# Nine masks and a copy in place of ten masks, and the mean subtracted inside ScalarE's squares and scalings, in a graph layer with residual and layer norm

## The chip, the cores and the metric

The kernel runs on one core of a Trainium2 chip. Five engines work side by side, each through its own list of instructions in order: PE (TensorE) multiplies and transposes, DVE (VectorE) and ACT (ScalarE) do elementwise work, POOL (GpSimd) here issues indirect DMAs (gathers and scatters), and SP (SyncE) issues the other DMAs. They wait for each other through semaphores. PE writes to PSUM, the others work from SBUF and PSUM. The metric is the time of one execution on the device in microseconds (us), as a median over runs.

## What is computed

50,000 nodes with 64 features, 25,000 edges sorted by target node, 10 edge types. All data is float32.

```
def ref(nfeat, efeat, relation_weight, res_fc_w, res_fc2_w, src, dst, etype):
    proj = einsum('ni,rio->nro', nfeat, relation_weight)
    t_r, h_r = proj[src, etype], proj[dst, etype]
    att = sum(t_r * tanh(h_r + efeat), axis=-1)
    a = softmax of att over the edges of each dst
    h_nb = segment_sum(nfeat[src] * a[:, None], dst)
    return leaky_relu((nfeat + h_nb) @ res_fc_w.T, 0.01) + leaky_relu(nfeat * h_nb @ res_fc2_w.T, 0.01)
y = x + ref(...)
return (y - mean(y)) / sqrt(var(y) + 1e-5)        # over the 64 features of a node
```

A node without edges has `h_nb` = 0, so its row needs only one product with `res_fc_w`.

## The kernel before

**Two kinds of work.** *Dense tiles*: all 50,000 rows are computed as if no node had edges, in 49 tiles of 1024 rows (128 partitions x 8 rows x 64 features = 128x512), and stored to `out`. *Edges*: the 25,000 edges lie in 196 columns of 128 and are handled in 25 steps of 8 columns (the last has 4). The rows of nodes that have edges ("finished rows") are then scattered over the dense ones.

**The loop.** Every engine runs the same loop, `s` from -1 to 28, written out by hand. In iteration `s`, PE, DVE and ACT treat: edge step `s` (transposing the gathered rows into `xT_ps`, masks, products with the weights: "quads"), edge step `e = s-1` (tanh, scores, softmax weights, running sums `es`), `f = s-2` (the two products of the output), `l = s-3` (norm of finished rows) and the dense tiles `3s+3` to `3s+5` (`D0`, `D1`, `D2`; `DP` is the last one of the iteration before). Tile 48, the last, is `D0` of iteration 15. ACT begins an iteration with the tanh of the edge step before.

**Masks and quads.** For each of the R = 10 types `r`, DVE's `mask(s, r)` (L963) writes `xm = (typ == r) * xT_ps`, 128x1024, into a ring of RM = 4; PE's `quad(s, r)` multiplies it with that type's weights, four products that add up in `t_ps` and `h_ps` over the ten types. `turn_in(s+1)` overwrites `xT_ps` when all masks of `s` are written.

**Norm of a dense tile.** PE transposes the tile (L566), ACT copies it (`dense_copy`, L712), PE multiplies (L573), ACT applies relu (`dense_relu`, L717), DVE adds (`dense_add`, L1025), sums over the 64 features (`dense_total`, L1030) and subtracts the mean (`dense_centre`, L1035). ACT squares (`dense_square`, L724: one 128x512 instruction), DVE sums (`dense_sum`, L1040). Once per iteration ACT takes the square roots of three tiles and one step of finished rows (`roots`, L777, with a table load before it and one behind it, L778), DVE inverts them (`inverse_roots`, L1047, semaphore `rec_done`), and ACT scales (`dense_norm`, L731: eight 128x64 instructions, since each row of a partition has its own factor). SP stores (L323). **Finished rows** go the same way in `final_sum`, `final_centre` (L1100), `final_square` (L783), `final_squares`, `final_out` (L790).

**POOL.** 384 gathers (L454), then, once all dense tiles are stored (`pool.wait_ge(o_stored[k], o_need(k))`), 196 scatters (L478), one gather for the node at the partitions' ends, and a last scatter (L495). Function `pace` puts waits ahead of some, so that gather number n is not issued before PE has done 14.6 n - 250 of its counted instructions (13.64 per scatter).

**SP.** Per iteration: types of the next step, edge features, loads of dense tiles (L317), stores of three tiles, the store of `es`, and 48 DMAs of single rows (L389, `rows_at`, six groups of eight) that replace some of POOL's gathers. All in one written order, so that a store also waits for the row DMAs ahead of it.

Of the kernel before, what the change touches and what calls it, by code (L numbers as in the profile page):

```python
# [5 lines left out]
ALU = mybir.AluOpType  # L6
# [17 lines left out]
RT = 2  # L24
# [5 lines left out]
RO = 3  # L30
RW = 18
# [9 lines left out]
def gnn_resnorm(nc, x, src, dst, eattr, etype, relw, resw, resw2, out):  # L41
# [55 lines left out]
    with ExitStack() as ctx:  # L97
# [9 lines left out]
        def sems(name, n):  # L107
# [35 lines left out]
        xm = sb("xm", [P, RM, COLS * P])  # L143
        ea = sb("ea", [P, RE, COLS, D])
# [49 lines left out]
        at_done = sem("at_done")  # L194
        typ_in = sems("typ_in", RT)
# [104 lines left out]
        def _(sp):  # L300
# [36 lines left out]
            def load_typ(s):  # L337
                if not 0 <= s < NS:
                    return
                wait(sp, masked, (s - RT + 1) * R)  # L340
# [162 lines left out]
        def _(pe):  # L503
# [12 lines left out]
            def turn_in(s):  # L516
# [3 lines left out]
                wait(pe, masked, s * R)  # L520
# [28 lines left out]
            def quad(s, r):  # L549
                pe.wait_ge(masked, s * R + r + 1)  # L550
                if r == 0:
                    wait(pe, prod_done, s)
                b = (s * R + r) % RM
                n = cols(s) // 2 * P
                for h in range(2):
                    pe.matmul(t_ps[h * D:(h + 1) * D, 0:n], w_rel[0:D, r, :], xm[0:D, b, h * n:(h + 1) * n],  # L556
                              start=(r == 0), stop=(r == R - 1), skip_group_check=True)
                    mm = pe.matmul(h_ps[(1 - h) * D:(2 - h) * D, 0:n], w_rel[D:P, r, :], xm[D:P, b, (1 - h) * n:(2 - h) * n],  # L558
                                   start=False, stop=(r == R - 1), skip_group_check=True)
                mm.then_inc(quad_done, 1)  # L560
# [62 lines left out]
            pe.wait_ge(setup_m, 3)  # L623
            for s in range(-1, LAST + 1):
# [45 lines left out]
                if s == NS:  # L670

                    pe.wait_ge(max_done, NS)
                    pe.wait_ge(masked, NS * R)
# [27 lines left out]
        def _(act):  # L701
# [6 lines left out]

            def dense_copy(d):
# [63 lines left out]
            def roots(s):  # L773
# [3 lines left out]
                act.activation(sd[:, s % 2, :, :], ssq[:, s % 2, :, :], ACT.Sqrt, scale=1.0 / D, bias=eps_t[:, 0:1]).then_inc(sqrt_done, 1)  # L777
# [508 lines left out]
```

## Time and profile before

| | us |
|---|---|
| median of 3 runs | 757.59 |
| lowest and highest | 756.48, 757.81 |
| the profiled execution | 757.37 |
| its span in the trace | 755.7 |
| busy in the span: DVE, POOL, PE, ACT | 628.0, 569.9, 567.3, 484.1 |
| mean granted clock of PE | 0.93 |

The profile is of one execution. Its page lists each engine's busy time, what each engine waited for ("idle before, releaser"), groups of instructions by source line, and the chain that ended last. A timeline lists instructions in order of time with start and duration; neighbours of one kind are merged (x8). An engine's successive instructions overlap a little, so that eight of 0.33 us can take 2.0 us. "PEclk" is the share of TensorE's full clock of 2.4 GHz that was granted; 0.50 is the lower level, 1.2 GHz.

### The profile page before, as it was taken

The numbers are of one execution on the slowest core, as the hardware profiler recorded it, in microseconds if no ns is written. First come the engines' busy times: TensorE is split into PE (matmuls) and PEld (weight loads), VectorE is DVE, ScalarE is ACT, GpSimd is POOL, SyncE is SP. The second block draws the span as 40 slices with busy tenths as digits, with TensorE's granted clock in tenths as the row PEclk, the third lists the DMA queues.
The fourth block names the chain that finished last, engine by engine and source line by source line (L and its number), as shares of the span: only waits on it lengthen the run. The fifth ranks groups of instructions, "written<-read, shape, count | busy, mean of one in ns | idle before, by whom it ended". The sixth has DMA issues, their size and how long they took to land. (4 is left out here: it accounts for less than half of the span.)

```text
span 755.7 us, 14910 instructions
## 1 busy us (share of the span) xinstructions
PE 567.3 (75%) x3948; PEld 310.8 (41%) x3948; DVE 628.0 (83%) x1118; ACT 484.1 (64%) x1432; POOL 569.9 (75%) x590
## 2 busy tenths in 40 slices
PE   1897888888888898888898796899988898853000
PEld 0652454454454454454454453444444443542000
DVE  2689899999999999999999999999998898862010
ACT  0376777778778788779779778655543555665040
POOL 6777777777777777777777777767777777777776
PEclk9999999999999999999999999999999999975555
DMA  4463434444434434434434424320222212100000
GB/s 120 112 188 83 122 99 138 113 110 137 124 100 138 124 96 139 124 97 141 134 85 147 113 56 123 98 77 28 76 76 74 75 37 80 45 27 18 18 18 16
DMA packets 49458, 70.44 MB, mean 93 GB/s; under 512 B 17450, under 2 KB 20966, under 8 KB 49374
## 3 DMA queue, kind: packets, MB, share of 16 engines
q1 hardware_dynamic: 30750, 52.33, 21.5%
q0 software_dynamic: 18624, 17.16, 11.0%
q8 instruction: 32, 0.52, 0.3%
q14 instruction: 52, 0.43, 0.2%
HBM read 45.61 MB, written 25.78 MB: 94 GB/s over the span
## 5 line engine op out<-in xcount | busy, mean ns | idle before, releaser
L454 POOL DMA_INDIRECT xsd<-in_x,ends_i x384 | 374.5, 975 | 118.0 <-issue 109.1
L556 PE MATMUL t_ps<-xm,w_rel 64*64 64x512 f32 (+1 forms) x1000 | 269.5, 621 | 42.0 <-DVE xm L963 41.2
L963 DVE SCALAR_TENSOR_TENSOR xm<-typ,xT_ps 128x1024 f32<-128x1024 f32 (+1 forms) x250 | 291.6, 1183 | 7.2 <-issue 7.2
L558 PE MATMUL h_ps<-xm,w_rel 64*64 64x512 f32 (+1 forms) x1000 | 269.5, 621 | 0.0
L478 POOL DMA_INDIRECT out<-out_r,row_i x196 | 192.3, 981 | 62.5 <-issue 56.7
L556 PEld LDWEIGHTS t_ps<-xm,w_rel 64*64 64x64 f32 x1000 | 52.8, 134 | 144.7 <-DVE xm L963 120.4
L573 PE MATMUL y_ps<-bd_cat,dT 128*128 128x256 f32 x392 | 97.0, 391 | 17.6 <-DVE zd L1025 14.9
L731 ACT ACTIVATE o_t<-zd,rstd 128x64 f32<-128x64 f32 x392 | 98.8, 337 | 15.4 <-DVE rstd L1047 15.3
L573 PEld LDWEIGHTS y_ps<-bd_cat,dT 128*128 128x128 f32 x392 | 71.8, 193 | 30.8 <-issue 12.9
L1005 DVE SCALAR_TENSOR_TENSOR es<-es,wd,wx 128x64 f32<-128x64 f32 x196 | 55.2, 281 | 11.2 <-DVE es L1005 0.5
L738 ACT ACTIVATE wd<-delta 128x16 f32<-128x16 f32 (+1 forms) x25 | 5.4, 216 | 88.2 <-DVE delta L993 83.8
L593 PEld LDWEIGHTS s_ps<-bd_both,uwT 128*128 128x128 f32 x224 | 29.6, 192 | 64.0 <-issue 51.9
L583 PE MATMUL tr_ps<-ident,uw 128*128 128x128 f32 x196 | 33.2, 294 | 26.4 <-DVE uw L1057 10.5
L558 PEld LDWEIGHTS h_ps<-xm,w_rel 64*64 64x64 f32 x1000 | 52.9, 134 | 0.0
L744 ACT ACTIVATE wx<-xsd,wd 128x64 f32<-128x64 f32 x196 | 52.1, 337 | 0.8
L593 PE MATMUL s_ps<-bd_both,uwT 128*128 128x128 f32 x224 | 39.8, 301 | 17.1 <-issue 17.1
L790 ACT ACTIVATE out_r<-zcf,rstd 128x64 f32<-128x64 f32 x196 | 49.1, 333 | 0.0
L583 PEld LDWEIGHTS tr_ps<-ident,uw 128*128 128x128 f32 x196 | 21.5, 145 | 65.4 <-issue 35.1
L1025 DVE TENSOR_TENSOR zd<-rd,y_ps 128x512 f32<-128x512 f32 x49 | 33.2, 677 | 9.2 <-ACT rd L717 9.2
L783 ACT ACTIVATE sqf<-zcf 128x512 f32<-128x512 f32 (+1 forms) x25 | 15.3, 613 | 39.6 <-DVE zcf L1100 39.5
L724 ACT ACTIVATE sqd<-zd 128x512 f32<-128x512 f32 x49 | 30.9, 631 | 12.6 <-DVE zd L1035 12.6
L777 ACT ACT_TABLE_LOAD x29 | 37.2, 1283 | 0.5
(155 smaller groups left out, 844.8 us busy)
## 6 DMA issues: line engine op xcount, KB each, us to landing
xsd<-in_x SPq DMA_DIRECT2D x1024, 0.2 KB
x_in<-in_x SPq DMA_DIRECT2D x48, 256.0 KB
typ<-typ_d SPq DMA_DIRECT2D x24, 512.0 KB, 4.8
out<-o_t SPq DMA_DIRECT2D x48, 256.0 KB
xsd<-in_x,ends_i POOLq DMA_INDIRECT x384
hist<-es SPq DMA_DIRECT2D x24, 256.0 KB, 2.0
ea<-in_edge_attr SPq DMA_DIRECT2D x24, 224.0 KB
out<-out_r,row_i POOLq DMA_INDIRECT x196, 2.1
```

The costliest lines, as they stand in the source:

```text
L454: pool.indirect_dma_start(xsd[:, s % RX, j, side, :], None, x[:, :], bass.IndirectOffsetOnAxis(ap=ends_i[:, side, c:c + 1], axis=0),).then ...
L478: pool.indirect_dma_start(out[:, :], bass.IndirectOffsetOnAxis(ap=row_i[:, c:c + 1], axis=0), out_r[:, s % RW, j, :], None, bounds_check=t ...
L556: pe.matmul(t_ps[h * D:(h + 1) * D, 0:n], w_rel[0:D, r, :], xm[0:D, b, h * n:(h + 1) * n], start=(r == 0), stop=(r == R - 1), skip_group_c ...
L558: mm = pe.matmul(h_ps[(1 - h) * D:(2 - h) * D, 0:n], w_rel[D:P, r, :], xm[D:P, b, (1 - h) * n:(2 - h) * n], start=False, stop=(r == R - 1) ...
L573: mm = pe.matmul(y_ps[:, j * 2 * P:(j + 1) * 2 * P], dT[:, d % 2, j * P:(j + 1) * P], bd_cat.rearrange("p k f -> p (k f)"), start=True, st ...
L583: mm = pe.transpose(tr_ps[:, j * P:(j + 1) * P], uw[:, g * QUAD + j, :, :].rearrange("p k f -> p (k f)"), ident[:, :])
L593: mm = pe.matmul(s_ps[:, YQ + j * P:YQ + (j + 1) * P], uwT[:, q // 2, k * P:(k + 1) * P], bd_both[:, :], start=True, stop=True)
L731: ins = act.activation(o_t[:, d % RO, j * D:(j + 1) * D], zd[:, d % RZ, j * D:(j + 1) * D], ACT.Copy, scale=rstd[:, s % 2, d % 3, j:j + 1])
L744: ins = act.activation(wx[:, j, :], xsd[:, e % RX, j, 0, :], ACT.Copy, scale=wd[:, e % 2, 0, j:j + 1])
L790: ins = act.activation(out_r[:, f % RW, j, :], zcf[:, f % 2, j, :], ACT.Copy, scale=rstd[:, s % 2, 3, j:j + 1])
L963: v.scalar_tensor_tensor(xm[:, (s * R + r) % RM, 0:n], typ[:, s % RT, 0:n], float(r), xT_ps[:, 0:n], ALU.is_equal, ALU.mult).then_inc(mask ...
L1005: v.scalar_tensor_tensor(es[:, e % RS, j, :], old, wd[:, e % 2, 1, j:j + 1], wx[:, j, :], ALU.mult, ALU.add).then_inc(chain_done, 1)
```

## The change

**Masks.** Since the ten masks add up to everything, sum over r of mask_r(x) W_r = x W_9 + sum over r < 9 of mask_r(x) (W_r - W_9). DVE subtracts W_9 from the other weights once in the setup (`dif_done`), writes nine masks, and ACT copies `xT_ps` whole to a new buffer `xc` (`plain`, right after tanh). PE still does ten quads; the one of `xc` stands at place 4. The first mask of a step now waits for ACT's copy.

**Norm.** `dense_centre` and `final_centre` are gone. The sums go to a table `zsum`. ACT's square becomes eight 128x64 instructions, (-64 z + sum)^2 with the sum as bias, and the root's scale goes from 1/D to 1/D^3. DVE gets a small `shifts` (-mean * rstd, 128x32), one mask after the reciprocal, and only it lets ACT go on (`rec_done`). ACT's scalings keep their number and form but take that as bias besides the scale. `zf` becomes a ring of three in place of `zcf`.

```
+            def plain(s):
+                n = cols(s) * P
+                act.wait_ge(xT_done, s + 1)
+                wait(act, quad_done, (s - 1) * R + PLAIN_AT + 1 if s > 0 else 0)
+                act.copy(xc[:, 0:n], xT_ps[:, 0:n]).then_inc(plain_done, 1)
             def dense_square(d):
-                act.wait_ge(zmid_done, d + 1)
+                act.wait_ge(zsum_done, d + 1)
                 wait(act, dred_done, d - 1)
-                act.activation(sqd[:, d % 2, :], zd[:, d % RZ, :], ACT.Square).then_inc(dsq_done, 1)
+                for j in range(DR):
+                    ins = act.activation(sqd[:, d % 2, j * D:(j + 1) * D], zd[:, d % RZ, j * D:(j + 1) * D], ACT.Square,
+                                         scale=-float(D), bias=zsum[:, d // 3 % 2, d % 3, j:j + 1])
+                ins.then_inc(dsq_done, 1)
             def dense_norm(d):
...
-                    ins = act.activation(o_t[:, d % RO, j * D:(j + 1) * D], zd[:, d % RZ, j * D:(j + 1) * D], ACT.Copy,
-                                         scale=rstd[:, s % 2, d % 3, j:j + 1])
+                    ins = act.activation(o_t[:, d % RO, j * D:(j + 1) * D], zd[:, d % RZ, j * D:(j + 1) * D], ACT.Identity,
+                                         scale=rstd[:, s % 2, d % 3, j:j + 1], bias=shift[:, s % 2, d % 3, j:j + 1])
...
             def final_square(f):
-                act.wait_ge(fsub_done, f + 1)
+                act.wait_ge(fsum_done, f + 1)
                 wait(act, red2_done, f)
-                act.activation(sqf[:, 0:cols(f), :], zcf[:, f % 2, 0:cols(f), :], ACT.Square).then_inc(fsq_done, 1)
+                for j in range(cols(f)):
+                    ins = act.activation(sqf[:, j, :], zf[:, f % RF, j, :], ACT.Square, scale=-float(D),
+                                         bias=zsum[:, f % 2, 3, j:j + 1])
+                ins.then_inc(fsq_done, 1)
...
+            v.tensor_tensor(w_rel[:, 0:RB, :], w_rel[:, 0:RB, :], w_rel[:, RB:R, :].to_broadcast([P, RB, D]), ALU.subtract).then_inc(dif_done, 1)
...
             def mask(s, r):
                 n = cols(s) * P
                 if r == 0:
-                    v.wait_ge(xT_done, s + 1)
+                    v.wait_ge(plain_done, s + 1)
...
-            def dense_centre(d):
-                v.wait_ge(zsum_done, d + 1)
-                z = zd[:, d % RZ, :].rearrange("p (j f) -> p j f", f=D)
-                v.scalar_tensor_tensor(z, zsd[:, :].unsqueeze(2).to_broadcast([P, DR, D]), -1.0 / D, z, ALU.mult, ALU.add).then_inc(zmid_done, 1)
...
-                v.reciprocal(rstd[:, s % 2, :, :], sd[:, s % 2, :, :]).then_inc(rec_done, 1)
+                v.reciprocal(rstd[:, s % 2, :, :], sd[:, s % 2, :, :]).then_inc(rstd_done, 1)
+
+            def shifts(s):
+                v.wait_ge(rstd_done, s + 1)
+                v.scalar_tensor_tensor(shift[:, s % 2, :, :], zsum[:, s % 2, :, :], -1.0 / D, rstd[:, s % 2, :, :],
+                                       ALU.mult, ALU.mult).then_inc(rec_done, 1)
```

The scaling of finished rows (`final_out`) changes as `dense_norm` does, and their sum and centring as those of the dense tiles.

How the instructions stand on ACT at the head of a dense iteration, from tanh to the exponent of the weights (`g_t` is tanh's output, `dT` the transposed tile, `h_t` the heads, `o_t` the scaled tile, `rd` the relu), before:

```order
L707 ACTIVATE g_t<-h_ps 128x512 [waits prod_done,quad_done]
L712 COPY dT<-tr_ps 128x512 [waits zadd_done,tr_in]
L756 ACTIVATE h_t<-es,rs 128x64 [waits uw_done,frec_done]
L756 ACTIVATE h_t<-es,rs 128x64 x3
L756 ACTIVATE h_t<-es,rs 128x64 [waits uw_done,frec_done]
L756 ACTIVATE h_t<-es,rs 128x64 x3
L731 ACTIVATE o_t<-zd,rstd 128x64 [waits o_stored2,rec_done]
L731 ACTIVATE o_t<-zd,rstd 128x64 x7
L717 ACTIVATE rd<-y_ps 128x512 [waits zadd_done,y_done]
L738 ACTIVATE wd<-delta 128x16 [waits den_done,delta_done]
```

and now:

```order
L722 ACTIVATE g_t<-h_ps 128x512 [waits prod_done,quad_done]
L728 COPY xc<-xT_ps 128x1024 [waits quad_done,xT_done]
L733 COPY dT<-tr_ps 128x512 [waits zadd_done,tr_in]
L780 ACTIVATE h_t<-es,rs 128x64 [waits uw_done,frec_done]
L780 ACTIVATE h_t<-es,rs 128x64 x3
L780 ACTIVATE h_t<-es,rs 128x64 [waits uw_done,frec_done]
L780 ACTIVATE h_t<-es,rs 128x64 x3
L755 ACTIVATE o_t<-zd,shift,rstd 128x64 [waits o_stored2,rec_done]
L755 ACTIVATE o_t<-zd,shift,rstd 128x64 x7
L738 ACTIVATE rd<-y_ps 128x512 [waits zadd_done,y_done]
L762 ACTIVATE wd<-delta 128x16 [waits den_done,delta_done]
```

The copy to `xc` is new in second place, and the scaling reads `shift` too. On ACT in the later half of the iteration, around the second scaling (`l` is a copy of PE's product, `sqd` and `sqf` are the squares), before:

```order
L712 COPY dT<-tr_ps 128x512 [waits zadd_done,tr_in]
L731 ACTIVATE o_t<-zd,rstd 128x64 [waits o_stored0,rec_done]
L731 ACTIVATE o_t<-zd,rstd 128x64 x7
L770 COPY l<-s_ps 128x256 [waits z1_done,y12_done]
L724 ACTIVATE sqd<-zd 128x512 [waits dred_done,zmid_done]
L783 ACTIVATE sqf<-zcf 128x512 [waits red2_done,fsub_done]
L717 ACTIVATE rd<-y_ps 128x512 [waits zadd_done,y_done]
```

and now:

```order
L733 COPY dT<-tr_ps 128x512 [waits zadd_done,tr_in]
L755 ACTIVATE o_t<-zd,shift,rstd 128x64 [waits o_stored0,rec_done]
L755 ACTIVATE o_t<-zd,shift,rstd 128x64 x7
L794 COPY l<-s_ps 128x256 [waits z1_done,y12_done]
L746 ACTIVATE sqd<-zd,zsum 128x64 [waits dred_done,zsum_done]
L746 ACTIVATE sqd<-zd,zsum 128x64 x7
L808 ACTIVATE sqf<-zf,zsum 128x64 [waits red2_done,fsum_done]
L808 ACTIVATE sqf<-zf,zsum 128x64 x7
L738 ACTIVATE rd<-y_ps 128x512 [waits zadd_done,y_done]
```

Each square is eight instructions where it was one. On DVE around the reciprocal of the roots, before:

```order
L963 SCALAR_TENSOR_TENSOR xm<-typ,xT_ps 128x1024 [waits quad_done]
L1005 SCALAR_TENSOR_TENSOR es<-es,wd,wx 128x64 [waits chain_done,wx_done] x2
L1047 RECIPROCAL rstd<-sd 128x32 [waits dmul_done,fmul_done,sqrt_done]
L963 SCALAR_TENSOR_TENSOR xm<-typ,xT_ps 128x1024 [waits quad_done]
L1035 SCALAR_TENSOR_TENSOR zd<-zsd,zd 128x512 [waits zsum_done]
L1100 SCALAR_TENSOR_TENSOR zcf<-zs,zf 128x512 [waits fmul_done,fsum_done]
```

and now:

```order
L997 SCALAR_TENSOR_TENSOR xm<-typ,xT_ps 128x1024 [waits quad_done]
L1039 SCALAR_TENSOR_TENSOR es<-es,wd,wx 128x64 [waits chain_done,wx_done] x2
L1079 RECIPROCAL rstd<-sd 128x32 [waits dmul_done,fmul_done,sqrt_done]
L997 SCALAR_TENSOR_TENSOR xm<-typ,xT_ps 128x1024 [waits quad_done]
L1083 SCALAR_TENSOR_TENSOR shift<-zsum,rstd 128x32 [waits rstd_done]
```

The two centrings behind the mask are gone, and `shift`, which ACT waits for, stands one mask behind the reciprocal.

## Rows read from the trace of the kernel before

**Rows 1.** The page: busy time, share of the span and instructions of each engine
```profile
PE 567.3 (75%) x3948; PEld 310.8 (41%) x3948; DVE 628.0 (83%) x1118; ACT 484.1 (64%) x1432; POOL 569.9 (75%) x590
```

**Rows 2.** Waits of POOL: what for, us in total, times, longest us
```profile
POOL xsd L454 <- issue: 109.1, 358, 0.3
```

**Rows 3.** Timeline of POOL: start us, us, engine, line, what; [idle before]
```profile
493.89 0.94 POOL L454 DMA_INDIRECT xsd<-in_x,ends_i  x1 [0.30 <-issue]
497.91 1.00 POOL L478 DMA_INDIRECT out<-out_r,row_i  x1 [3.07 <-DMA out<-o_t]
...
751.24 0.97 POOL L495 DMA_INDIRECT out<-out_fix,fix_i  x1 [0.30 <-issue]
```

**Rows 4.** Timeline of ACT, stages 15 and 16
```profile
468.00 2.02 ACT L731 ACTIVATE o_t<-zd,rstd 128x64 f32<-128x64 f32 x8
...
470.32 0.60 ACT L707 ACTIVATE g_t<-h_ps 128x512 f32<-128x512 f32 x1
```

**Rows 5.** Timeline of SP, stage 16
```profile
494.47 0.74 SPq L323 DMA_DIRECT2D out<-o_t  x2
```

**Rows 6.** Windows: us, busy (instructions) of each engine, PEclk, DMA share, GB/s
```profile
303.83:332.01 28.18, 23.71 (x167) 13.08 (x165) 27.57 (x48) 22.89 (x70) 21.47 (x23) 1.00 0.44 120
...
582.00:583.00 1.00, 1.00 (x8) 0.30 (x8) 1.00 (x2) 0.00 (x0) 0.70 (x2) 0.50 0.00 1
```

**Rows 7.** Timeline of ACT, stage 10, from one tanh to the next
```profile
303.09 0.60 ACT L707 ACTIVATE g_t<-h_ps 128x512 f32<-128x512 f32 x1 [0.30 <-PE h_ps L558]
...
306.93 2.00 ACT L731 ACTIVATE o_t<-zd,rstd 128x64 f32<-128x64 f32 x8
...
312.52 0.22 ACT L738 ACTIVATE wd<-delta 128x16 f32<-128x16 f32 x1 [2.89 <-DVE delta L993]
...
314.33 0.63 ACT L724 ACTIVATE sqd<-zd 128x512 f32<-128x512 f32 x1 [0.49 <-DVE zd L1035]
314.86 2.00 ACT L790 ACTIVATE out_r<-zcf,rstd 128x64 f32<-128x64 f32 x8
...
323.26 2.02 ACT L731 ACTIVATE o_t<-zd,rstd 128x64 f32<-128x64 f32 x8 [0.60 <-DVE rstd L1047]
...
331.29 0.60 ACT L707 ACTIVATE g_t<-h_ps 128x512 f32<-128x512 f32 x1 [0.30 <-PE h_ps L558]
```

**Rows 8.** Timeline of DVE, stage 10
```profile
316.48 0.68 DVE L1040 TENSOR_REDUCE ssq<-sqd 128x8 f32<-128x512 f32 x1
...
322.88 0.34 DVE L1047 RECIPROCAL rstd<-sd 128x32 f32<-128x32 f32 x1
```

**Rows 9.** Groups by form: count | busy us, mean ns of one | idle before
```profile
L963 DVE SCALAR_TENSOR_TENSOR xm<-typ,xT_ps 128x1024 f32<-128x1024 f32 x240 | 285.1, 1204 | 7.2 <-issue 7.2
...
L1035 DVE SCALAR_TENSOR_TENSOR zd<-zsd,zd 128x512 f32<-128x512 f32 x49 | 33.6, 685 | 0.6
...
L731 ACT ACTIVATE o_t<-zd,rstd 128x64 f32<-128x64 f32 x392 | 98.8, 337 | 15.4 <-DVE rstd L1047 15.3
...
L712 ACT COPY dT<-tr_ps 128x512 f32<-128x512 f32 x49 | 28.6, 584 | 12.9 <-PE tr_ps L566 12.7 <-DVE zd L1025 0.2
...
L770 ACT COPY l<-s_ps 128x256 f32<-128x256 f32 x56 | 19.8, 354 | 0.0
...
L778 ACT ACTIVATE fix<-eps_t 128x1 f32<-128x1 f32 x29 | 5.9, 203 | 0.3
...
L856 ACT ACTIVATE fix<-fix 128x1 f32<-128x1 f32 x1 | 0.3, 280 | 0.0
...
L803 ACT COPY xfix<-xsd 128x64 f32<-128x64 f32 x1 | 0.2, 244 | 0.3 <-PE xT_ps L524 0.3
```

**Rows 10.** Timeline of ACT: the tanh that ends stages 0, 4 and 14
```profile
51.58 0.60 ACT L707 ACTIVATE g_t<-h_ps 128x512 f32<-128x512 f32 x1 [0.45 <-PE h_ps L558]
...
161.78 0.60 ACT L707 ACTIVATE g_t<-h_ps 128x512 f32<-128x512 f32 x1 [0.24 <-PE h_ps L558]
...
444.01 0.60 ACT L707 ACTIVATE g_t<-h_ps 128x512 f32<-128x512 f32 x1 [0.29 <-PE h_ps L558]
```

More of the change, by code:

```diff
@@ L30 @@
 RO = 3
+RF = 3
 RW = 18
@@ L80, in gnn_resnorm, with quad_count @@
             TR_DENSE[d], tr_uses = tr_uses, tr_uses + 1
+    RB = R - 1
+    PLAIN_AT = 4
+    def quad_count(m):
+        return m // RB * R + m % RB + (2 if m % RB >= PLAIN_AT else 1)
     LATE = (ND - 1) // 3 - 2
@@ L339, in load_typ @@
                     return
-                wait(sp, masked, (s - RT + 1) * R)
+                wait(sp, masked, (s - RT + 1) * RB)
                 n = cols(s) * P
@@ L519, in turn_in @@
                     pe.wait_ge(rows_in[ROW_BLOCKS.index(s)], P * DMA)
-                wait(pe, masked, s * R)
+                wait(pe, masked, s * RB)
                 half = cols(s) // 2
@@ L547, in add_edges, with quad @@
                 mm.then_inc(eadd_done, 1)
-            def quad(s, r):
-                pe.wait_ge(masked, s * R + r + 1)
-                if r == 0:
+            def quad(s, at):
+                plain = at == PLAIN_AT
+                r = RB if plain else at - (at > PLAIN_AT)
+                if plain:
+                    pe.wait_ge(plain_done, s + 1)
+                else:
+                    pe.wait_ge(masked, s * RB + r + 1)
+                if at == 0:
                     wait(pe, prod_done, s)
-                b = (s * R + r) % RM
                 n = cols(s) // 2 * P
+                moving = xc[:, :] if plain else xm[:, (s * RB + r) % RM, :]
+                w = w_rel[:, r, :]
                 for h in range(2):
[L556 to L559, printed above, removed]
+                    pe.matmul(t_ps[h * D:(h + 1) * D, 0:n], w[0:D, :], moving[0:D, h * n:(h + 1) * n],
+                              start=(at == 0), stop=(at == R - 1), skip_group_check=True)
+                    mm = pe.matmul(h_ps[(1 - h) * D:(2 - h) * D, 0:n], w[D:P, :], moving[D:P, (1 - h) * n:(2 - h) * n],
+                                   start=False, stop=(at == R - 1), skip_group_check=True)
                 mm.then_inc(quad_done, 1)
@@ L776, in roots @@
                 wait(act, rec_done, s - 1)
[L777 removed]
+                act.activation(sd[:, s % 2, :, :], ssq[:, s % 2, :, :], ACT.Sqrt, scale=1.0 / D ** 3, bias=eps_t[:, 0:1]).then_inc(sqrt_done, 1)
                 act.activation(fix[:, 15:16], eps_t[:, 0:1], ACT.Exp)
             def final_square(f):
[L781 removed]
+                act.wait_ge(fsum_done, f + 1)
                 wait(act, red2_done, f)
[L783 removed]
+                for j in range(cols(f)):
+                    ins = act.activation(sqf[:, j, :], zf[:, f % RF, j, :], ACT.Square, scale=-float(D),
+                                         bias=zsum[:, f % 2, 3, j:j + 1])
+                ins.then_inc(fsq_done, 1)
             def final_out(f, s):
@@ L789, in final_out @@
                 for j in range(cols(f)):
-                    ins = act.activation(out_r[:, f % RW, j, :], zcf[:, f % 2, j, :], ACT.Copy, scale=rstd[:, s % 2, 3, j:j + 1])
+                    ins = act.activation(out_r[:, f % RW, j, :], zf[:, f % RF, j, :], ACT.Identity,
+                                         scale=rstd[:, s % 2, 3, j:j + 1], bias=shift[:, s % 2, 3, j:j + 1])
                 ins.then_inc(fmul_done, 1)
@@ L1134, in _ @@
                     pair(f)
-                if DP is not None:
-                    dense_centre(DP)
                 if main:
                     mask(s, 4)
-                if main:
-                    mask(s, 5)
                 if DP is not None:
@@ L1148, in _ @@
                 if main:
-                    mask(s, 6)
+                    mask(s, 5)
                 if on:
@@ L1157, in _ @@
                 if main:
-                    mask(s, 7)
+                    mask(s, 6)
                 if on:
@@ L1164, in _ @@
                 if main:
-                    mask(s, 8)
-                if D0 is not None:
-                    dense_centre(D0)
-                if late:
-                    final_centre(l)
+                    mask(s, 7)
+                if s >= 0:
+                    shifts(s)
                 if on:
@@ L1173, in _ @@
                 if main:
-                    mask(s, 9)
+                    mask(s, 8)
                 if D1 is not None:
@@ L1178, in _ @@
                     dense_total(D1)
-                if D1 is not None:
-                    dense_centre(D1)
                 if late:
```

56 lines of the change are left out of this document (32 added, 24 removed).

## The prediction

> **What bounds the kernel now.** I read the page's table of busy times first [rows 1]: DVE 83%, POOL 75%, PE 75%, ACT 64%. It misleads twice. POOL's quarter of idle time is no slack: its waits are nearly all the 0.3 us that it spends between two indirect DMAs whatever else happens (358 such, none longer) [rows 2]. So POOL issues one DMA every 1.25 to 1.28 us from 3.6 us to the end, and the chain that ended last is POOL alone. It really waits once. Its last gather ends at 494.83, and its first scatter starts at 497.91, after 3.07 us of waiting for the last dense store [rows 3], since scattered rows may overwrite dense ones. From there 196 scatters and the fix run to 752.21, and the span ends at 755.7; the profiled run took 757.37 (span plus 1.67), 0.22 below the median of 757.59.
>
> The end therefore hangs on one time: when the last dense tile (48) is stored. SP issues that store at 494.47 [rows 5]. In SP's order 24 gathers of single rows, the loads of the next stage, a store and 16 more row DMAs stand between the second-last pair of stores and it, and that pair waited for the scaling that ended at 470.02 [rows 4]. So tile 48 leaves 24.4 us after ACT is through stage 15: the dense stages set it, one after another. I call stage s the stretch from tanh(s-1) to tanh(s) on ACT.
>
> One dense stage [rows 6, 7]: 28.18 us, of which DVE is busy 27.57, PE 23.71, ACT 22.89. DVE bounds it. ACT's idle time is not spread: it waits 2.89 us for `delta` before the exponent and else 0.49, 0.60 and 0.30 us [rows 7].
>
> **What DVE gives up.** Per dense stage one mask of 1.20, three dense centrings and one of finished rows of 0.69 [rows 9]. Overlapping its neighbour each is about 0.08 less, so 1.12 + 4 x 0.61 = 3.6. It gets one tiny `shifts` (bound from below by nothing, from above by the 0.34 of the reciprocal of equal size [rows 8]; I take 0.2). DVE alone would do a stage in 24.8.
>
> **What ACT gets.** Four pieces, none covered, since ACT's one long wait lies elsewhere:
> - Squares. A run of eight 64-wide activations takes 2.02 us, and the next work starts 1.93 after its start; a 512-wide square takes 0.63, the next starts 0.53 after it [rows 7]. Each of the four squares (three dense, one of finished rows) grows by 1.40: 5.6 us.
> - The second operand. Scaling used one vector operand (scale) and now has two (scale and bias). No row shows an activation with two. A 64-wide copy without any takes 244 ns, the scaled one 337 [rows 9]: 93 ns for a scale. A one-column Exp takes 203 without and 280 with a vector bias [rows 9]: 77 ns for a bias. Bounds for the second one: 0 (it is read beside the first) and 93. The two nearest rows each charge for theirs, so I take 91: a run of eight scalings grows by 0.73, and there are four such runs (three dense, one of finished rows).
> - `xc`, a 1024-wide copy out of PSUM. 512 columns take 584 ns, 256 take 354 [rows 9]; the slope gives 1.04, 0.94 net. It lies between tanh and the exponent.
> - The waits. ACT now feeds DVE's first mask: copy at about 1.5 us after tanh, DVE reaches the mask at 3.7 or later, so nothing.
>
> The Trainium skill ("ScalarE: Activation LUTs", section "What ACT_TABLE_LOAD costs") gives 186 ns + 0.833 ns a column, 93 ns more for each vector operand and an overlap of 93 ns between neighbours. The one-operand rows agree (337 and 244); the two-operand case no row here shows, and by the page it would be the upper bound. The same page's table of rules sends adds and multiplies to VectorE, which speaks against this change.
>
> **The new stage.** ACT's work has two parts. From tanh to the exponent it is not ACT's own: product, sums, four masks and the scores on DVE must pass, 312.52 - 303.09 = 9.43 [rows 7]. None of these is removed. In a stage that waits for ACT the product starts as soon as tanh ends, 0.1 sooner: 9.3. ACT's own work there (tanh, `xc`, copy, heads, scaling, relu) becomes 7.0 and stays hidden, so `xc` and one of the four scalings cost nothing. From the exponent to the next tanh everything is ACT's: 331.29 - 312.52 = 18.77, less its three waits of 1.39 [rows 7], is 17.38. Add 5.6 for squares and 3 x 0.73 for scalings: 25.15. Sum: 9.3 + 25.15 = **34.45 us**, against 28.2.
>
> Does another wait come last in it? The scaling needs `rec_done`. The sum of the last tile's squares now waits for ACT: square done at 9.3 + 1.22 + 2.02 = 12.55; from that sum to the reciprocal's end DVE takes 323.22 - 316.48 = 6.74 [rows 8] with two masks in it both before and after; then one mask (1.2) and `shifts`: 20.7. ACT gets there at 9.3 + 9.65 + 1.40 + 0.73 = 21.1. No wait, by 0.4. By my walk through PE's order it has its last multiplication and transposes done 1 to 2 us before tanh.
>
> **The sum over stages.**
> - Setup: subtracting one weight from nine (576 columns) stands on DVE before the types' copy: +0.7.
> - Stage 0: two squares 2.8, two scalings 1.5, and the second square now waits for the relu and sum behind it: +4.8.
> - Stages 1 to 4: before 161.78 - 51.58 = 110.2 [rows 10]. Stages 3 and 4 have no scaling of finished rows, so ACT comes early and waits for `rec_done`: 20.7 + 13.35 = 34.05 each. Stage 2 lacks the square of finished rows too, and stage 1 all work on finished edges: 30.8 and 31.3. Together 130.2: +20.0.
> - Stages 5 to 14: 10 x 34.45 = 344.5 against 444.01 - 161.78 = 282.2 [rows 10]: +62.3.
> - Stage 15: one dense tile; it has two copies, two relus and a square less (3.9): 30.6 against 470.32 - 444.01 = 26.3 [rows 4, 10]: +4.3.
> - From there SP's 24.4 us and POOL's 254.3 us stay. POOL's gathers have rules to stay near PE's progress; they will wait there, but end before the store.
>
> Sum 92.1. 757.37 + 92.1 = **849.5 us**.
>
> **The rivals.**
> 1. *The second operand is free.* The stage is then bound by `rec_done`: 20.7 + 11.95 = 32.65, and the sum changes: 10 stages give +44.3, stages 1 to 4 +14, stage 0 +3.3, stage 15 +2.7, setup 0.7: 65. Time **822**. For it: no row with two operands. Against: each costs alone. Chance 0.2.
> 2. *PE falls to its lower clock.* Now PE has 10.7 us idle per stage, some in one piece: it will wait about 3.7 us for `uwT` in front of the second transposition of pairs. Before, the granted clock was 0.50 (1.2 GHz) at 582 to 583 [rows 6], after PE had been idle for some 2.5 us, and 1.00 through stage 10. A few us at half speed cost about 2, and PE has about 2 to give; I price it at 1 per stage over 14 stages: **863**. Chance 0.12.
> 3. *ACT does not become the bound (not slower).* If a run of eight small squares and scalings costs little more than one 512-wide, ACT stays below 28.2, DVE sets 24.8, the last store lands early and POOL is alone the bound: 3.07 becomes 0.30, nothing else can move, **754.6**, faster by 0.37%. It decides at 1.5 us of work added behind the exponent (9.3 + 17.4 = 26.7 against 28.2); I count 7.8. Against it stands the 2.02 us of a run of the same width. Chance 0.02.
>
> **How the numbers follow.** My sum 0.62, the rivals 0.2, 0.12 and 0.02, the rest (an unseen wait on either side) 0.04. The range 816 to 868 takes in both bounds of the operand and the clock. Faster than before by over 0.2%, about what a measurement of this kernel can tell from no change, 0.02; within it 0.01; slower 0.97.
>
> **What would show it.** In the changed profile a dense stage of 34.4 us with ACT busy some 32 and one wait of 2.3 us before the exponent; runs of eight squares at 2.0 and of scalings at 2.8 us, one scaling at 0.43; DVE below 24 us in a stage, now waiting for tanh and relu; the first scatter near 590, after a wait of some 10 us; from there 254 us as before. The forecast is wrong if the two-operand activation takes 0.34, if stages show ACT idle after the exponent, or if the scatters wait for anything of their own.

## The result: 844.4 us, and the profile after

The changed kernel takes **844.38 us** (median of 4 runs, 843.6 to 846.83). The kernel before, run beside it, takes 757.7 (756.48 to 758.19). The ratio is 1.1148, with a 95% interval of 1.1135 to 1.1162. The profiled run took 843.6 us with a span of 841.9. The forecast was 849.5, slower.

The page's busy times, where [rows 1] stand before:

```profile
PE 603.0 (72%) x3948; PEld 341.7 (41%) x3948; DVE 565.8 (67%) x1050; ACT 655.6 (78%) x1971; POOL 572.6 (68%) x590
```

DVE gave up 62 us and ACT took on 171. The next row is a window over one dense stage, stage 11; its columns are those of [rows 6]:

```profile
390.87:425.08 34.21, 26.36 (x164) 15.40 (x164) 24.54 (x42) 31.88 (x101) 21.24 (x22) 0.90 0.36 100
```

34.21 us in place of 28.18, with ACT busy 31.88 and nobody else above 26.4. ACT's timeline of that stage, as [rows 7] before (start, duration, line, tiles, idle before):

```profile
390.87 0.60 ACT L722 ACTIVATE g_t<-h_ps 128x512 f32<-128x512 f32 x1
391.34 1.01 ACT L728 COPY xc<-xT_ps 128x1024 f32<-128x1024 f32 x1
...
394.63 2.78 ACT L755 ACTIVATE o_t<-zd,shift,rstd 128x64 f32<-128x64 f32 x8
398.23 0.60 ACT L738 ACTIVATE rd<-y_ps 128x512 f32<-128x512 f32 x1 [0.82 <-PE y_ps L587]
400.25 0.21 ACT L762 ACTIVATE wd<-delta 128x16 f32<-128x16 f32 x1 [1.42 <-DVE delta L1027]
...
401.46 2.00 ACT L746 ACTIVATE sqd<-zd,zsum 128x64 f32<-128x64 f32 x8
403.37 2.75 ACT L817 ACTIVATE out_r<-zf,shift,rstd 128x64 f32<-128x64 f32 x8
...
411.81 2.76 ACT L755 ACTIVATE o_t<-zd,shift,rstd 128x64 f32<-128x64 f32 x8
...
424.60 0.59 ACT L738 ACTIVATE rd<-y_ps 128x512 f32<-128x512 f32 x1
425.08 0.59 ACT L722 ACTIVATE g_t<-h_ps 128x512 f32<-128x512 f32 x1
```

No row from 400.49 to 425.08 has a bracket: ACT works without a gap from the exponent to the next tanh. Its only idle time, 0.82 + 1.42 us, stands ahead of the exponent. A run of eight squares takes 2.00 and one of scalings 2.76. One instruction of each, from the groups by form (compare the 337 in [rows 9]):

```profile
L755 ACT ACTIVATE o_t<-zd,shift,rstd 128x64 f32<-128x64 f32 x392 | 135.7, 441 | 11.0 <-DVE shift L1083 10.9
L746 ACT ACTIVATE sqd<-zd,zsum 128x64 f32<-128x64 f32 x392 | 98.9, 340 | 1.6 <-DVE zsum L1066 1.6
L817 ACT ACTIVATE out_r<-zf,shift,rstd 128x64 f32<-128x64 f32 x196 | 67.3, 425 | 0.0
```

DVE now waits for ACT: in the same stage it has one gap of almost six us. The first row is from its timeline, the second the sum over the run from the table of waits (us, times, longest):

```profile
419.16 0.69 DVE L1059 TENSOR_TENSOR zd<-rd,y_ps 128x512 f32<-128x512 f32 x1 [5.94 <-ACT rd L738]
```

```profile
DVE zd L1059 <- ACT rd L738: 92.3, 17, 7.4
```

The end, as in [rows 3] and [rows 5]: POOL's last gather and first scatter, then SP's store of tile 48.

```profile
575.57 0.95 POOL L462 DMA_INDIRECT xsd<-in_x,ends_i  x1 [0.30 <-issue]
585.65 1.00 POOL L486 DMA_INDIRECT out<-out_r,row_i  x1 [9.14 <-DMA out<-o_t]
```

```profile
582.40 0.73 SPq L331 DMA_DIRECT2D out<-o_t  x2
```

The wait is 9.14 in place of 3.07. The store leaves 87.93 us later than before (582.40 against 494.47) and the run takes 86.2 longer.

### The profile page after: what moved, and what is told of

Read it like the earlier page. It is cut to its first block and busy times, and to the rows that moved or that the text cites. A ratio compares the mean times of both kernels' runs of the same rounds, so it can differ in the third digit from the quotient of the medians.

```text
span 841.9 us, 15472 instructions
## 1 busy us (share of the span) xinstructions
PE 603.0 (72%) x3948; PEld 341.7 (41%) x3948; DVE 565.8 (67%) x1050; ACT 655.6 (78%) x1971; POOL 572.6 (68%) x590
## 3 DMA queue, kind: packets, MB, share of 16 engines
q1 hardware_dynamic: 30750, 52.33, 19.5%
## 5 line engine op out<-in xcount | busy, mean ns | idle before, releaser
L997 DVE SCALAR_TENSOR_TENSOR xm<-typ,xT_ps 128x1024 f32<-128x1024 f32 (+1 forms) x225 | 264.1, 1184 | 1.3 <-ACT xc L728 0.7
L570 PE MATMUL t_ps<-xm,w_rel 64*64 64x512 f32 (+1 forms) x900 | 243.7, 636 | 12.6 <-DVE xm L997 11.9
L572 PE MATMUL h_ps<-xm,w_rel 64*64 64x512 f32 (+1 forms) x900 | 243.7, 636 | 0.0
L755 ACT ACTIVATE o_t<-zd,shift,rstd 128x64 f32<-128x64 f32 x392 | 135.7, 441 | 11.0 <-DVE shift L1083 10.9
L587 PE MATMUL y_ps<-bd_cat,dT 128*128 128x256 f32 x392 | 120.8, 463 | 27.6 <-DVE zd L1059 24.0
L587 PEld LDWEIGHTS y_ps<-bd_cat,dT 128*128 128x128 f32 x392 | 87.8, 235 | 46.8 <-issue 17.1
L746 ACT ACTIVATE sqd<-zd,zsum 128x64 f32<-128x64 f32 x392 | 98.9, 340 | 1.6 <-DVE zsum L1066 1.6
L570 PEld LDWEIGHTS t_ps<-xm,w_rel 64*64 64x64 f32 x900 | 52.4, 139 | 99.3 <-issue 49.5
L817 ACT ACTIVATE out_r<-zf,shift,rstd 128x64 f32<-128x64 f32 x196 | 67.3, 425 | 0.0
L808 ACT ACTIVATE sqf<-zf,zsum 128x64 f32<-128x64 f32 x196 | 49.2, 336 | 18.0 <-DVE zsum L1135 18.0
L1072 DVE TENSOR_REDUCE ssq<-sqd 128x8 f32<-128x512 f32 x49 | 32.1, 680 | 17.0 <-ACT sqd L746 17.0
```

Source lines behind the costliest of these rows:

```text
L570: pe.matmul(t_ps[h * D:(h + 1) * D, 0:n], w[0:D, :], moving[0:D, h * n:(h + 1) * n], start=(at == 0), stop=(at == R - 1), skip_group_check ...
L572: mm = pe.matmul(h_ps[(1 - h) * D:(2 - h) * D, 0:n], w[D:P, :], moving[D:P, (1 - h) * n:(2 - h) * n], start=False, stop=(at == R - 1), ski ...
L587: mm = pe.matmul(y_ps[:, j * 2 * P:(j + 1) * 2 * P], dT[:, d % 2, j * P:(j + 1) * P], bd_cat.rearrange("p k f -> p (k f)"), start=True, st ...
L746: ins = act.activation(sqd[:, d % 2, j * D:(j + 1) * D], zd[:, d % RZ, j * D:(j + 1) * D], ACT.Square, scale=-float(D), bias=zsum[:, d // ...
L817: ins = act.activation(out_r[:, f % RW, j, :], zf[:, f % RF, j, :], ACT.Identity, scale=rstd[:, s % 2, 3, j:j + 1], bias=shift[:, s % 2, 3 ...
L997: v.scalar_tensor_tensor(xm[:, m % RM, 0:n], typ[:, s % RT, 0:n], float(r), xT_ps[:, 0:n], ALU.is_equal, ALU.mult).then_inc(masked, 1)
```

## The experiments

Twelve runs follow, of eight edited kernels (four of them ran twice), in three batches on three chips. On the second batch's chip the kernel before took 758.1 us, as in the result. On the first's it took 920.75 and on the third's 910.02; what those traces still tell is said below. My theory is the one of the forecast: two edits of ACT's norm (small squares, a second operand) make the stretch from exponent to tanh ACT's own, and the end follows the last dense store. The rivals were that the nine masks do it, that one of the two edits of the norm alone does, or that ACT's total busy time counts, wherever the work stands.

**Norm alone.** The changed kernel with the ten masks of before; shown against it:

```
-                if 0 <= s < NS:
-                    plain(s)
...
-            v.tensor_tensor(w_rel[:, 0:RB, :], w_rel[:, 0:RB, :], w_rel[:, RB:R, :].to_broadcast([P, RB, D]), ALU.subtract).then_inc(dif_done, 1)
...
+                if main:
+                    mask(s, 5)
```

> Again only the mean taken off in ACT's squares and scalings, with ten masks. Where before takes 757 us: dense stage 34.2 us, first scatter at 585, 844 us (842 to 845). Rival (the copy xc costs 0.94 us a stage): 830. Rival (loss shared by both halves): 800 or less.

Measured 845.65 (845.12 to 846.71), ratio 1.1161 (1.1144 to 1.1178). Stages 5 to 14 take 34.15 to 34.17 us, as those of the whole change. DVE has one mask more and ACT no `xc` copy, and neither changes the stage. The copy's place shows as a longer wait ahead of the exponent: 3.10 us in a stage, 2.19 with the copy. So the whole loss is the norm's.

**Masks alone.** The kernel before with nine masks and the copy `xc`; shown against the changed kernel, whose norm is put back as it was before:

```
-                                         scale=-float(D), bias=zsum[:, d // 3 % 2, d % 3, j:j + 1])
...
+                act.activation(sqd[:, d % 2, :], zd[:, d % RZ, :], ACT.Square).then_inc(dsq_done, 1)
...
+                v.scalar_tensor_tensor(z, zsd[:, :].unsqueeze(2).to_broadcast([P, DR, D]), -1.0 / D, z, ALU.mult, ALU.add).then_inc(zmid_done, 1)
```

> Again only nine masks and ACT's copy xc, the norm as before, since in the first set all kernels, the one before among them, took 920 us and the edits could not be told apart. Where the kernel before takes 757 us I expect: POOL alone the bound, first scatter at 495 us in place of 498, 754.8 us, 0.37% below before. Rival (the stages are the bound): 741. Rival (the copy costs what the mask gives): 757.6. If before takes 920 us again, no difference.

Measured 756.61 (755.2 to 759.25, 11 runs) against 758.1, ratio 0.9976 (0.9965 to 0.9988): faster by 1.5 us, the one version that beats both kernels. The mechanism at the end is as expected. POOL goes from its last gather to its first scatter without a wait:

```profile
497.73 0.95 POOL L462 DMA_INDIRECT xsd<-in_x,ends_i  x1 [0.30 <-issue]
498.98 1.02 POOL L486 DMA_INDIRECT out<-out_r,row_i  x1 [0.30 <-issue]
```

The store of tile 48 is now issued at 489.40, 5.1 us earlier. In this profiled run (759.25, the longest of the eleven) the gathers took 985 ns on the mean where the profile of before, from an earlier run, has 975, which is 3.8 us over 384 of them and eats the 2.77 of the wait; the median says that most runs keep part of it. Half of the expected 3.3 us came.

What failed is my 27.1 us for the stage. A window over stage 10 and two waits of ACT and two of DVE in it:

```profile
298.27:326.83 28.56, 25.16 (x165) 13.93 (x165) 26.77 (x46) 23.93 (x71) 21.84 (x23) 0.94 0.41 119
```

```profile
298.27 0.61 ACT L722 ACTIVATE g_t<-h_ps 128x512 f32<-128x512 f32 x1 [0.45 <-PE h_ps L572]
299.26 1.01 ACT L728 COPY xc<-xT_ps 128x1024 f32<-128x1024 f32 x1 [0.39 <-PE xT_ps L532]
```

```profile
321.49 0.69 DVE L1051 TENSOR_TENSOR zd<-rd,y_ps 128x512 f32<-128x512 f32 x1 [0.32 <-ACT rd L738]
...
325.18 1.23 DVE L1089 SCALAR_TENSOR_TENSOR l<-l 128x1024 f32<-128x1024 f32 x1 [0.58 <-ACT l L791]
```

DVE is busy 26.77 in place of 27.57 [rows 6], yet stages 5 to 14 take 28.10 to 28.57, no less than before, and DVE, ACT and PE each wait a little for one another. What holds the stage is a ring through all three. It is seen best in stage 12, where PE kept its clock (start, duration and wait of the rows that hand over):

```profile
355.39:383.50 28.11, 23.66 (x165) 13.10 (x166) 26.73 (x46) 23.93 (x72) 21.39 (x23) 1.00 0.41 121
```

```profile
356.02 0.69 DVE L996 TENSOR_TENSOR prod<-t_ps,g_t 128x512 f32<-128x512 f32 x1 [0.33 <-ACT g_t L722]
...
365.82 0.68 DVE L1061 SCALAR_TENSOR_TENSOR zd<-zsd,zd 128x512 f32<-128x512 f32 x1
```

```profile
366.53 0.63 ACT L745 ACTIVATE sqd<-zd 128x512 f32<-128x512 f32 x1 [0.49 <-DVE zd L1061]
...
374.04 0.35 ACT L791 COPY l<-s_ps 128x256 f32<-128x256 f32 x1
```

```profile
374.49 0.68 PE L607 MATMUL s_ps<-bd_both,uwT 128*128 128x128 f32 x4 [1.06 <-issue]
```

```profile
383.50 0.60 ACT L722 ACTIVATE g_t<-h_ps 128x512 f32<-128x512 f32 x1 [0.45 <-PE h_ps L572]
```

Tanh lets DVE begin the product, and DVE works without a gap up to the centring, which ends at 366.50. That lets ACT's square go, and ACT works without a gap up to its first copy `l`, which ends at 374.39. In the code PE's next pair of products waits for that copy (`pf_done`; the row itself names nobody), and from 374.49 PE works without a gap up to the heads that the next tanh waits for. The trace of before has the same ring, with tanh at 303.09, ACT's square at 314.33 and the next tanh at 331.29 [rows 7]:

```profile
313.61 0.68 DVE L1035 SCALAR_TENSOR_TENSOR zd<-zsd,zd 128x512 f32<-128x512 f32 x1
```

```profile
321.82 0.35 ACT L770 COPY l<-s_ps 128x256 f32<-128x256 f32 x1
```

```profile
322.28 0.68 PE L593 MATMUL s_ps<-bd_both,uwT 128*128 128x128 f32 x4 [1.06 <-issue]
```

But there DVE has no wait from one tanh to the next either, so DVE and the ring were bounds within about 0.1 us of each other. The mask that is gone stood behind the centring, outside the ring, so the ring kept its 28.1.

PE's clock explains the rest. In the four stages of 28.10 to 28.23 us (5, 6, 9, 12) the granted clock is 1.00, in the six of 28.54 to 28.57 it is 0.94, as in stage 10 above. There PE had been idle for 2.06 us until 312.57, and from 314 to 317 it was granted 0.50 (1.2 GHz):

```profile
315.00:316.00 1.00, 1.00 (x7) 1.00 (x6) 1.00 (x2) 0.97 (x3) 0.69 (x2) 0.50 0.92 279
```

Its second pair of products then starts 19.55 us after tanh where stage 12 has 19.10, and the stage is longer by the same 0.45. All ten stages have those 2.06 us of idleness and four of them kept the clock, so what decides it the rows don't show.

The store came early all the same: stages 0 to 4, where less is in flight, were 5.0 us shorter in sum (stage 5 begins at 156.73, before at 161.78), stages 5 to 14 gave 1.6 of that back, and stage 15, with one dense tile, shrank from 26.3 to 24.7.

**No second operand.** The changed kernel with scalings that take the scale alone, without the bias:

```
-                    ins = act.activation(o_t[:, d % RO, j * D:(j + 1) * D], zd[:, d % RZ, j * D:(j + 1) * D], ACT.Identity,
-                                         scale=rstd[:, s % 2, d % 3, j:j + 1], bias=shift[:, s % 2, d % 3, j:j + 1])
+                    ins = act.activation(o_t[:, d % RO, j * D:(j + 1) * D], zd[:, d % RZ, j * D:(j + 1) * D], ACT.Copy,
+                                         scale=rstd[:, s % 2, d % 3, j:j + 1])
```

> Again the changed kernel without the bias in the scalings (the mean is not taken off in the output). Where before takes 757 us: stage 32.5 us in place of 34.17, bound by the wait for rec_done, 819 us. Rival (second operand free in time): 844. Rival (no wait comes in): 800.

Measured 820.4 (820.02 to 821.32), ratio 1.0822 (1.0805 to 1.0838). Here the wait of my forecast's first rival shows, in each of the stages: ACT is early at the scaling and waits for DVE's small `shifts`.

```profile
396.88 2.02 ACT L755 ACTIVATE o_t<-zd,rstd 128x64 f32<-128x64 f32 x8 [0.28 <-DVE shift L1083]
...
408.67 0.59 ACT L722 ACTIVATE g_t<-h_ps 128x512 f32<-128x512 f32 x1
```

Stages 5 to 14 take 32.34 to 32.39 and 32.66 to 32.97 by turns. In the longer ones the granted clock is 0.84 to 0.90 in place of 0.95, and tanh waits 0.21 to 0.29 us for PE. My rival 1 had 32.65 and 822. Undoing the operand gives back 24.0 us (844.4 - 820.4).

**Whole squares.** The changed kernel with 512-wide squares, which leave the mean out:

```
-                for j in range(DR):
-                    ins = act.activation(sqd[:, d % 2, j * D:(j + 1) * D], zd[:, d % RZ, j * D:(j + 1) * D], ACT.Square,
-                                         scale=-float(D), bias=zsum[:, d // 3 % 2, d % 3, j:j + 1])
-                ins.then_inc(dsq_done, 1)
+                act.activation(sqd[:, d % 2, :], zd[:, d % RZ, :], ACT.Square, scale=float(D)).then_inc(dsq_done, 1)
```

> Again the changed kernel with 512-wide squares without bias (the mean is left out of the variance). Where before takes 757 us: stage 28.65 us, 764 us (760 to 770). Rival (ACT's last wait is for DVE's rec_done, not its own work): 829.

Measured 769.08 (768.24 to 770.88), ratio 1.0143 (1.0127 to 1.0158). Undoing the small squares gives back 75.3 us. Stages take 28.93 to 29.27 where 28.65 was expected: the exponent comes 9.65 to 9.70 us after tanh in nine of the ten, not 9.33. With squares this short DVE is no longer through with the stage before when tanh ends. In stage 12 tanh begins at 371.43, and the product stands behind DVE's own `zf`:

```profile
371.81 0.69 DVE L1100 TENSOR_TENSOR zf<-l 128x512 f32<-128x512 f32 x1
372.42 0.68 DVE L998 TENSOR_TENSOR prod<-t_ps,g_t 128x512 f32<-128x512 f32 x1
```

It starts 0.99 us after tanh, where in the changed kernel it starts 0.62 after (391.49 against 390.87). The exponent is later by about as much.

The two undone edits add up to 99.3 us, more than the 87.8 by which masks alone and the whole change lie apart (844.4 - 756.6). They needn't agree: below some length of the stages another bound takes over, the ring of 28.1 in masks alone (which has the centring back on DVE), and POOL for the end. With both undone and no centring the shares would give a stage of 34.2 - 5.6 - 2.2 = 26.4. Whether it gets there isn't shown; that kernel ran only on the chip of the third batch (below).

**The same four on another chip.** The same kernels had run in the first batch:

| | this chip (before 920.75) | ratio, 95% interval |
|---|---|---|
| masks alone | 921.72 | 1.0022 (0.9994 to 1.0051) |
| norm alone | 922.83 | 1.0051 (1.0012 to 1.009) |
| no second operand | 919.67 | 0.9985 (0.9949 to 1.0021) |
| whole squares | 919.83 | 0.9967 (0.9927 to 1.0007) |

> Only the second half: ten masks as before, the mean taken off in ACT's squares and scalings. My theory: all of the slowdown is here, since ACT sets the stage: dense stage 34.2 us as in the changed kernel, DVE has room for the tenth mask and ACT's copy was hidden, so 844 us (842 to 845), first scatter at 585 us. Rival (the copy xc costs 0.94 us in each of 15 stages): 830 us. Rival (the loss is shared by both halves, because masks now wait for ACT): 800 us or less.

Nothing of the 11% shows there; all four expectations failed in their absolute numbers, as the one above does. POOL's timeline (masks alone) tells what is different. Its DMAs take 0.97 us as on the other chip, but every few of them there is a gap of over 1 us, also in the scatters:

```profile
713.49 0.97 POOL L486 DMA_INDIRECT out<-out_r,row_i  x1 [0.30 <-issue]
715.91 0.97 POOL L486 DMA_INDIRECT out<-out_r,row_i  x1 [1.45 <-PE h_ps L572]
717.19 0.97 POOL L486 DMA_INDIRECT out<-out_r,row_i  x1 [0.30 <-issue]
```

Masks alone needed 252.8 us from the first scatter to the last on the usual chip (498.98 to 751.80) and 297.8 here (614.92 to 912.69). Among its 384 gathers one gap was longer than 0.5 us there, and 96 are here, 132.6 us in sum. For 70.9 us of them (49 gaps) the trace gives "remote", which names no engine. The rest may be true waits: by `pace` gathers and scatters wait for PE's progress, and each step's scatters wait for ACT's finished rows (once for 8.59 us here). The other engines have gaps too, so that POOL's show a slow kernel and needn't be the cause. In the traces of this and of the third batch's chip, whatever the edit, stages 5 to 14 take 34.5 to 35.6 us on the mean (masks alone 35.2, norm alone 35.1). The stages of the kernel before, as far as such a trace has them (store first, below), take 34.6 us on the mean, of which ACT idles some 11. The changed kernel's stage of 34.2 us finds room in that, and so norm alone costs almost nothing. What makes the gaps the traces don't show.

**Extra work on ACT, in two places.** Two 512-wide copies in stages 1 to 15 of the changed kernel, in one version ahead of the exponent (next to `heads`), in the other behind it:

```
+            def extra(e):
...
+                for k in range(2):
+                    ins = act.copy(xc2[:, k, :], w_rel[:, 0:8, :].rearrange("p r f -> p (r f)"))
+                ins.then_inc(extra_done, 1)
```

> The changed kernel with two more 512-wide copies on ACT (a copy of a weight table that nobody reads, about 1.06 us by the 584 ns of a 512-wide copy and the overlap of neighbours) in each of stages 1 to 15, between tanh and the exponent; the ring of finished rows is 16 instead of 18 to make room. My theory: ACT has some 7 us of work there in 9.3 us that belong to DVE's delta, and waits 2.2 us in a stage; the copies are hidden in that wait: 844 to 846 us. Rival: ACT's busy time as a whole sets the stage, so that any work on it counts wherever it stands: 15 x 1.06 = 16 us more, 860.

> The same two copies on ACT in the same stages, but behind the exponent, after the first run of small squares. My theory: from the exponent to the next tanh everything is ACT's own, so each of the 10 stages with finished rows and the last one grows by 1.06 (11 x 1.06 = 11.7 us), and in stages 1 to 4 ACT waits for the reciprocal anyway, so that most of it is hidden there: 856 us. Rivals: ACT's busy time as a whole counts, then this and the kernel with the copies ahead of the exponent both take 860; or ACT is not the bound, then both stay at 844.5.

This batch again ran on a chip with gaps (before 910.02). Copies ahead: 917.91 (914.06 to 921.09), ratio 1.0112 (1.0035 to 1.019). Copies behind: 930.47 (919.44 to 931.91), 1.0229 (1.0139 to 1.032). The absolute numbers missed with the chip, and the intervals overlap. But some stages have no gap in them, and there the place can be read. ACT's timeline, copies ahead, stage 12, up to the exponent (the extra copies are the `x2` row; it leaves out the number of their buffer `xc2`):

```profile
444.95 0.59 ACT L724 ACTIVATE g_t<-h_ps 128x512 f32<-128x512 f32 x1
...
446.80 1.16 ACT L736 COPY xc<-w_rel 128x512 f32<-128x512 f32 x2
...
454.28 0.21 ACT L771 ACTIVATE wd<-delta 128x16 f32<-128x16 f32 x1 [1.28 <-DVE delta L1038]
...
479.20 0.58 ACT L724 ACTIVATE g_t<-h_ps 128x512 f32<-128x512 f32 x1
```

The exponent stands 9.33 us after tanh, as without the copies. They came out of the wait, now 1.28 instead of 2.19 to 2.24, and the stage takes 34.25. Copies behind, stage 9:

```profile
343.73 0.60 ACT L724 ACTIVATE g_t<-h_ps 128x512 f32<-128x512 f32 x1
...
353.11 0.21 ACT L771 ACTIVATE wd<-delta 128x16 f32<-128x16 f32 x1 [1.15 <-DVE delta L1038]
...
356.23 1.12 ACT L736 COPY xc<-w_rel 128x512 f32<-128x512 f32 x2
...
378.97 0.59 ACT L724 ACTIVATE g_t<-h_ps 128x512 f32<-128x512 f32 x1
```

35.24 us: 1.07 longer than 34.17. Of that 1.03 are the two copies (the next work starts at 357.26), the rest is an exponent that comes 0.05 later. The wait ahead of the exponent is 2.23, as ever. Eight of the ten stages take 35.56 to 35.70 with one gap of 0.24 to 0.39 in them. So of one and the same work next to nothing counts in one place and all of it in the other, in the one undisturbed stage of each kernel that is shown. ACT's busy time as a whole is not the rule, which settles the rival for the stage; for the time of the whole kernel it has only the disturbed runs.

**Neither squares nor operand.** Both of the edits above at once:

> The changed kernel without ACT's mean: squares are 512-wide again and the scalings take no bias, so the mean is left out of the variance and of the output (nine masks stay, DVE still makes the shift). My theory: the two terms (squares 5.6, second operand 2.2 a stage) are all that makes ACT the bound. Without both, DVE's work sets about 25 to 27 us a stage, the last dense store lands before POOL's last gather ends, and POOL alone sets the end, as in the kernel with nine masks and DVE's mean: 756, within 755 to 757.5. Rival: with a shorter dense stage POOL has more to give and the time goes on falling with the stages (16 x 1.5 us less): 732.

Measured 912.19 (903.95 to 916.58) where before took 910.02, ratio 1.0051 (1.0008 to 1.0094). On this chip it can't be told whether it would fall to 756 or lower. It is not 22 us faster than before, as the rival had it (732 against 758), but on a chip where the gaps set the pace that says little. Inconclusive.

**Store first.** The kernel before, with SP's store of tile 48 in iteration 16 moved ahead of the last 16 row DMAs that it stood behind (24 and 8 more still stand before it):

```
                 load_x(d + 4)
+                if s == 16:
+                    store_o(48)
                 rows_at((s - 1) * PER_STEP + 1)
```

> The kernel before with one edit: in SP's order of iteration 16 the store of the last dense tile (48) stands ahead of the row DMAs and the loads that it stood behind. My theory: the 3.07 us that POOL waits in front of its first scatter is the only time in which POOL is not issuing, so the store, landing several us earlier, takes at most 2.8 us off: 755.3 where the kernel before takes 758.1. Rival: the rows and loads that now come later behind the store hold up stage 16 or the gathers by as much, and nothing changes or it gets slower.

Measured 904.48 (898.06 to 907.48, 12 runs), ratio 0.9977 (0.9937 to 1.0017). POOL's wait before the first scatter is shorter than in the other three kernels of this chip (4.31 here, 9.75 with neither, 9.86 and 10.47 with the copies). Those are changed kernels, though; the wait of before itself was not traced on this chip:

```profile
598.61 1.00 POOL L481 DMA_INDIRECT out<-out_r,row_i  x1 [4.31 <-DMA out<-o_t]
```

The direction is the expected one, but the interval takes in no change, so nothing is shown. On a chip without gaps it was not tried.

## Why the forecast was right, and where it was off

It was 5.9 us too high (849.5 against the profiled 843.6; 5.1 against the median). Its steps, against the trace of after:

| step | forecast | measured |
|---|---|---|
| setup and stage 0 | +5.5 | +4.6 (56.16 - 51.58) |
| stages 1 to 4 | +20.0 | +19.5 (129.7) |
| stages 5 to 14 | +62.3 | +59.5 (341.7) |
| stage 15 | +4.3 | +4.3 (30.6) |
| SP's path from the last tanh to the store | 0 | +0.1 (24.24) |
| from the store to the end | 0 | -1.7 (259.5 against 261.2) |

- **POOL bounds the end, and the last dense store starts it:** held. Masks alone took the wait away, and the long wait of 9.14 came as forecast ("some 10 us"). POOL's gathers now wait for PE's progress (47.3 us for `y_ps`, 32 times) and still end 9 us early.
- **From DVE to ACT:** held, in all four pieces. Squares: 2.00 to 2.04 a run, as taken. The second operand, which no row of before showed: a run of eight takes 2.74 to 2.79 where it took 2.00 to 2.03, so about 0.75 against my 0.73. Single ones take 425 and 441 ns against 337. The Trainium skill ("ScalarE: Activation LUTs", section "What ACT_TABLE_LOAD costs") gives 93 ns for each vector operand, and the trace agrees, with 88 to 104. My choice of the upper bound was right, and the experiment without the operand gave the other end (820.4 where rival 1 had 822).
- **Work ahead of the exponent is free:** held: +0.0 for `xc` (norm alone), +0.1 for two extra copies, against +1.07 behind the exponent. The exponent comes 9.33 to 9.38 us after tanh; I had 9.3.
- **From exponent to tanh:** 24.83 us, forecast 25.15. This is the term that was mis-sized: 0.3 in each of ten stages, 2.8 us in all. I subtracted ACT's three waits of 1.39 from 18.77, but where a wait goes, the next instruction also begins under the end of the one before, by some 0.1 us, and I had left those three overlaps out. In [rows 7] and their like a start comes 0.1 before its neighbour's end only where no bracket stands.
- **`rec_done` not last, by 0.4:** held, by 0.3. `shift` ended at 411.50 and the scaling began at 411.81. In stage 3 and 4 it did come last (33.86 and 33.85 us; forecast 34.05).
- **Setup and stage 0:** 0.9 too high. The subtraction pushed ACT's first copy back by 0.44 (18.13 to 18.57), not 0.7, and ACT's waits for DVE's centring in stage 0 shrank with the centring itself (the first from 1.36 to 0.63), a gain that I hadn't counted.
- **The tail:** I held it fixed. The 196 scatters took 973 ns each on the mean, where before they took 981 (1.6 us).
- **PE's clock:** the granted clock did fall, from 1.00 to 0.90 over the dense stage. In stage 11 PE idles 3.34 us in front of the second transposition of pairs (forecast 3.7), until 406.73, and from 408 to 411 it is granted 0.50. It did not set the stage: ACT had no wait for PE behind the exponent. Rival 2 had the fall and not the cost. In kernels with shorter stages the fall did cost something, 0.45 us in a stage of masks alone and 0.3 without the second operand.
- **"DVE bounds it" (the dense stage of before):** half right. DVE has a single wait there in stages 5 to 14 (0.27 us), but the ring described under masks alone is within 0.1 us of it. That did no harm to the sum, which goes by ACT's own work. The 24.8 us of DVE alone, to which rival 3 would have let the stage fall, and the 27.1 that I expected of masks alone overlooked the ring: with DVE lighter, the stage stays at 28.1 and more.

## What to carry to other kernels

Split a stage at the wait that an engine can't avoid, and price moved work by the side on which it lands: here two copies (1.04 us) cost 0.1 ahead of the exponent and 1.07 behind it. A 512-wide square took 0.63 us and eight 64-wide ones over the same data 2.00, so a constant that changes every 64 columns costs ACT more (1.4 us) than the pass on DVE that it saves (0.6). Before giving an engine relief, ask what the end hangs on: taking the masks alone gave 0.2%, because only a wait of 3 us was to be had. And look for the path that passes through several engines: a mask of 1.2 us less on the busiest one left the stage as long as it was, since the mask stood outside the ring.

## What the runs showed of the chip beyond that

- The time differs between chips by more than any of these edits made. The kernel before took 757.7 and 758.1 us in two measurements, and 910.0 and 920.8 on two other chips. Each chip was measured at one time only, so whether the chip or the time makes the difference isn't shown. In the slow ones POOL's own work takes as long as elsewhere (0.97 us a scatter), but the engines have gaps between their instructions (on POOL mostly of 1 to 2 us). SP takes longer for its row DMAs: masks alone needs 12.65, 14.79 and 19.97 us for the three groups of 24 around the end of the dense stages, against 9.92, 9.87 and 9.42 on the usual chip. There an edit worth 11% elsewhere was worth 0.5%. The two single undisturbed stages shown are still within 0.1 us of what the other traces give.
- The clock granted to PE can differ from stage to stage in one run of one program: in masks alone it is 1.00 in four dense stages and 0.94 in six, with the same 2 us of idleness ahead.
- An indirect DMA's mean duration on POOL differs by 1% between profiles: gathers 975 ns before and 986 after, scatters 981 before and 973 after. Over 384 gathers 11 ns are 4.2 us, more than the 1.5 us that the nine masks gave.
